# A piece of quantised weights, three fills and two splits change places in the order of work of a four-layer kernel

## What is computed

```python
# layer 0: matrix memory attention, q = layernorm(x), k = v = context
itilde = einsum(gate_in, Wi_w) + Wi_b
ftilde = einsum(gate_in, Wf_w) + Wf_b
csum   = cumsum(log_sigmoid(ftilde))
Dtilde = (csum[i] - csum[j], masked) + itilde[j]
D      = exp(Dtilde - max(Dtilde))
C      = (q @ k.T) * D / TAU
H      = (C @ v) / (max(|sum(C)|, exp(-max)) + 1e-6)
x      = x + tanh(g) * groupnorm(H)
# layer 1, feed-forward: three weight matrices, quantised in blocks of 32 to 4 bits and back
s  = max(|w|) / 7 ;  wq = round(w / s) * s
# layer 2 and 3: attention with 16 heads of 8, whose operands are split into f16 parts
```

## Time and profile before

| | us |
|---|---|
| median of 3 runs | 549.97 (548.64 to 550.31) |
| the profiled execution, its own time | 548.92 |
| the span of that execution, first to last instruction | 546.8 |
| mean granted clock of TensorE | 0.874 |
| critical chain: share of PE, DVE, ACT, POOL | 49%, 27%, 9%, 7% |

### The profile page before, as it was taken

One profiled execution on the slowest core, in us unless ns is written; L12 is line 12 of the kernel. 1 busy time (PEld: TensorE's weight loads), 2 busy tenths in 40 slices (PEclk: granted clock), 3 DMA queues, 4 the chain that ended last, 5 costly groups with the idle time before them and its releaser, 6 DMA issues.

```text
span 546.8 us, 11355 instructions
## 1 busy us (share of the span) xinstructions
PE 421.6 (77%) x4145; PEld 264.0 (48%) x4145; DVE 382.1 (70%) x1061; ACT 320.0 (59%) x656; POOL 234.1 (43%) x364
## 2 busy tenths in 40 slices
PE   3637754999895680049999989986999998889886
PEld 3524421656563330035655666663456656666432
DVE  7766994866876767867666675978786687586441
ACT  2339973656453167247876767663576568778250
POOL 4613896365766908226311111344845662311100
PEclk9999885999998585569999978787899999889787
DMA  7840006400000000000000000000000000000000
GB/s 205 200 36 2 2 2 201 94 1 2 1 1 0 1 0 0 0 1 2 1 2 1 3 2 2 1 2 1 2 1 0 3 1 2 1 3 1 2 19 19
DMA packets 26001, 11.27 MB, mean 21 GB/s; under 512 B 16358, under 2 KB 22876, under 8 KB 25948
## 3 DMA queue, kind: packets, MB, share of 16 engines
q1 hardware_dynamic: 25948, 10.56, 7.8%
HBM read 10.03 MB, written 0.52 MB: 19 GB/s over the span
## 4 chain that ended last, share of the span: by engine, by line
PE 49%; DVE 27%; ACT 9%; POOL 7%; issue 5%; SPq 1%; DMA 1%; DVEq 0%; ACTq 0%
PE psum L709 10%; PE psum L891 6%; PE psum L876 4%; PE psum L877 4%; PE psum L878 3%; DVE qs L1704 3%; POOL work L638 2%; PE psum L1073 2%; PE psum L1007 2%; ACT phase L1098 2%; POOL rstd L566 2%; DVE z L1319 2%; PE psum L716 2%; PE psum L982 2%; ACT phase L1272 2%
## 5 line engine op out<-in xcount | busy, mean ns | idle before, releaser
L638 POOL TENSOR_TENSOR work<-work 128x512 f16<-128x512 f32 x64 | 72.8, 1161 | 43.9 <-ACT work L1158 43.8
L564 POOL TENSOR_SCALAR vr<-mv 128x1 f32<-128x1 f32 x80 | 17.9, 223 | 158.1 <-DVE mv L1313 157.2
L1704 DVE TENSOR_REDUCE qs<-psum 128x4 f16<-128x512 f32 x96 | 59.6, 688 | 7.8 <-PE psum L982 7.7
L1098 ACT ACTIVATE phase<-psum 128x1024 f16<-128x1024 f16 (+1 forms) x52 | 47.5, 933 | 19.3 <-PE psum L709 10.5
L1213 ACT ACTIVATE work<-psum 128x512 f32<-128x512 f32 x64 | 37.5, 596 | 35.7 <-PE psum L878 31.0
L1596 DVE TENSOR_TENSOR work<-work,psum 128x512 f32<-128x512 f32 x64 | 42.7, 684 | 18.5 <-ACT work L1213 16.1
L1272 ACT ACTIVATE phase<-psum 128x512 f32<-128x512 f32 x96 | 49.8, 610 | 4.8 <-PE psum L1007 4.1
L876 PE MATMUL psum<-zTh,split 128*128 128x512 f16 x128 | 51.1, 399 | 1.4 <-POOL zTl L643 1.0
L891 PE MATMUL psum<-wout,work 128*128 128x128 f16 x768 | 47.7, 219 | 4.5 <-POOL work L638 4.2
L877 PE MATMUL psum<-zTl,split 128*128 128x512 f16 x128 | 51.1, 399 | 0.0
L878 PE MATMUL psum<-zTh,split 128*128 128x512 f16 x128 | 51.0, 398 | 0.0
(11 more groups left out here) (339 smaller groups left out, 973.9 us busy)
## 6 DMA issues: line engine op xcount, KB each, us to landing
stage_f<-in_L_ffn_W_in SPq DMA_DIRECT2D x1, 2048.0 KB, 9.5
stage_f<-in_L_ffn_w SPq DMA_DIRECT2D x1, 2048.0 KB, 8.7
x<-in_x SPq DMA_DIRECT2D x1, 512.0 KB, 4.2
c<-in_ctx SPq DMA_DIRECT2D x1, 512.0 KB, 5.5
w<-in_L_ffn_W SPq DMA_DIRECT2D x2, 256.0 KB
out<-x SPq DMA_DIRECT2D x8, 64.0 KB, 1.6
phase<-in_L_ffn_w_up SPq DMA_DIRECT2D x1, 192.0 KB
phase<-in_L_ffn_w_gate SPq DMA_DIRECT2D x1, 192.0 KB
```

The costliest lines, as they stand in the source:

```text
L638: ch.do(pool.tensor_tensor(hidl[:, n % 2, k, :], act[:, n % 2, k, :], hidh[:, n % 2, k, :], ALU.subtract), sem("hid_low"))
L1098: ch.do(A(out, view(u), ACT.Copy), banks.freed(stage, b, name))
L1704: ch.do(v.tensor_reduce(groups(qs[:, b, :, 3 * DA:3 * DA + 1], 4)[:, j], u, AX.X, ALU.max, negate=True), free_of(stage, b, f"s{j}"))
```

## The change

The third item of w8 gets turn 3.7 in place of 2, which puts it behind `x0_score 1`. `x0_split` becomes a chain of its own, with items 0 and 1 ahead of `x0_forget`. The three fills of `qs` and `ks` move from `x0_split 0` to the setup, ahead of the fills of `magic` and `ones`.

```diff
+    "xs": ["x0_split"],
-    "x0": ["x0_split", "x0_stack", "x0_score", "x0_value", "x0_back", "x0_group", "f0_z", "f0_t"],
+    "x0": ["x0_stack", "x0_score", "x0_value", "x0_back", "x0_group", "f0_z", "f0_t"],
...
-    "w8": [(i, i, 0) for i in range(3)],
+    "w8": [(0, 0, 0), (1, 1, 0), (2, 3.7, 0)], "xs": [(0, -0.36, 0), (1, -0.34, 0)] + [(b, b, 0) for b in range(2, NB)],
...
+                    ch.do(v.memset(qs[:, :, :, 3 * DA:4 * DA], 0.0))
+                    ch.do(v.memset(ks[:, :, :, 3 * DA + 1:4 * DA], 0.0))
+                    ch.do(v.memset(ks[:, :, :, 3 * DA:3 * DA + 1], 1.0), sem("stacks_filled"))
                     ch.do(v.memset(magic[:, :], MAGIC))
                     ch.do(v.memset(ones[:, :], 1.0), sem("ones_ready"))
                 elif stage == "x0_split":
-                    if b == 0:
-                        ch.do(v.memset(qs[:, :, :, 3 * DA:4 * DA], 0.0))
-                        ch.do(v.memset(ks[:, :, :, 3 * DA + 1:4 * DA], 0.0))
-                        ch.do(v.memset(ks[:, :, :, 3 * DA:3 * DA + 1], 1.0), sem("stacks_filled"))
```

More of the change, by code:

```diff
@@ L77 @@
     "s0": [(e, e, 0) for e in range(NE)], "so": [(e, e, 0) for e in range(NE)], "s2": [(e, e, 0) for e in range(NE)],
-    "w8": [(i, i, 0) for i in range(3)], "u1": [((c, g), FPS * c + g, 0) for c in range(3) for g in range(FPS)],
+    "w8": [(0, 0, 0), (1, 1, 0), (2, 3.7, 0)], "xs": [(0, -0.36, 0), (1, -0.34, 0)] + [(b, b, 0) for b in range(2, NB)], "u1": [((c, g), FPS * c + g, 0) for c in range(3) for g in range(FPS)],
 }
@@ L112 @@
 }
-PERIOD = {"n0": 1.0, "s0": 0.9, "w8": 1.29, "x0": 1.0, "s2": 1.26, "f0": 1.5,
+PERIOD = {"n0": 1.0, "s0": 0.9, "w8": 1.29, "x0": 1.0, "xs": 1.0, "s2": 1.26, "f0": 1.5,
           "so": 0.5, "x1": 0.38, "u1": 0.62, "x2": 1.26, "f2": 1.95, "x3": 1.44}
```

## The result

The changed kernel is slower: 552.81 us (median of 20 executions) against 549.25 (20), ratio 1.0082, 95% interval 1.0052 to 1.0113. That is 4.5 us by the ratio and 3.6 by the medians; 4.1 were forecast. The profiled execution has a span of 551.6 us, 4.8 more than the one of before.

The account below looks back on a forecast made before the run. It took a chain of waits in the first 60 us as the bound, no engine being full. 0.95 + 0.03 + 2.6 + 1.5 - 1.0 = 4.1 us over the median 549.97 gave 554.1, range 551.5 to 556.1.

Parts of the forecast that it names:

- the likeliest case: Whole kernel: the delay as worked out, 3.4 to 5.4 us, thus 553.4 to 555.4; chance 0.75.
- Fills: At the setup: the moved fills shift statistics and gates by 1.8 us, bounds 0 to 1.8, covered by the load.
- Splits: Ahead of x0_forget on DVE: two splits, 1.3 us, fit into its 1.68 us wait for PE and cost nothing there.
- 3.6 us of cover: Ahead of the biases: slack 39.8 - 36.2 that hides the shifts from early fills and splits.
- more: Stacks 1 and 2: low clock lasts or the two shifts outgrow the cover; 6 us, 556.0, chance 0.08.
- The load as floor: Step w1 on PE: its last load holds the biases, so they gain only 1.0 us, bounds 0 to 1.3.
- The price of the piece: Between score 1 and stack 2: the piece takes DVE 2.6 us, then 1.5 to ACT's stack, bounds 1.1 to 1.85.
- It reaches the end: Behind stack 2: ACT, DVE and POOL have no slack, so the full 4.1 us goes to the end.
- The rival that the load is no floor: Step w1: the load lands before 34 us, the gain is 4.9, the sum -0.2, time 549.8; chance 0.03.
- g: At the biases: the gain in their start, limited by the load; taken as 1.0 us, bounds 0 to 1.3.
- The rival that DVE's idle time soaks the piece up: Around score 1: DVE's idle 1.48 + 1.20 us absorbs the piece's 2.6, leaving the 1.0 gain; 549.0, chance 0.08.
- The receipt: Last load of step w1: a receipt behind the last byte, most of about 2 us, would bring the gain nearer 0.

Follow-up runs that it names:

- e2: The second experiment: the kernel before with only the third w8 piece moved behind score 1, fills and splits unmoved; 554.49 us against 547.62, ratio 1.0136.
- e1: The first experiment: the changed kernel with the third weight piece back at turn 2, fills and splits still early; 549.41 us against 547.62 for before.
- e4: The changed kernel with step w1 (transpose, product needing the load, bias rows) behind the first block's groups; 550.89 us against 547.62 for before, ratio 0.9968.
- e3: The changed kernel with the third piece's DVE work back at turn 2 and only its transpose late; 547.47 us against 547.62 for before, ratio 0.9979.
- e5: The changed kernel with the third piece's DVE work at turn 2, its transpose late and step w1 late; 546.31 us against 548.19 for before, ratio 0.9965.
- e7: The changed kernel with throwaway PE matmuls, 5 in the wait for the load and 10 in the wait for the third piece; 551.06 us against 548.19 for before.
- e8: The changed kernel run again without any edit; 552.89 us against 548.19 for before, ratio 1.0089.
- e6: The changed kernel with the third piece's DVE work at turn 2, its transpose, step w1 and the fills late; 543.72 us against 548.19 for before.

## Why the prediction was right

Its forecast of 554.1 was 4.1 over before; measured is 4.5 by the ratio, within the likeliest case's 3.4 to 5.4. The median itself, 552.81, lies 1.3 under the forecast: inside the range of 551.5 to 556.1, but under the 553.4 at which the likeliest case began, since before has a median of 549.25 over 20 executions and not 549.97. The chances for slower add up to 0.89, not to the 0.88 that it gives.

At stack 2 its sum can be redone with what was measured: 0.95 + 0.03 + 2.61 + 1.90 - 0.92 = 4.57, where it had 0.95 + 0.03 + 2.6 + 1.5 - 1.0 = 4.1. Two sizes were off. The hand-over behind the piece was 0.4 larger. The gain at the load was 0.8 larger at the biases, but had shrunk to 0.92 by the end of score 1, and that this is so near the 1.0 taken is luck. Point by point:

- **Fills.** 1.8 us taken, 2.03 measured at the statistics (6.20 to 8.23). Hidden by the load, as said: in the changed kernel PE still waited 2.38 us for it. The second experiment agrees, without early fills and splits its last norm lies 0.10 from that of the changed kernel. The 0.05 us of the first says nothing on this, since the load ends no wait there.
- **Splits.** `x0_forget` was forecast at 21.3 and came at 21.51. The gates were done near 21.0 on PE, but DVE came out of the first piece 2.4 us later than before and not 1.8 (20.17 against 17.78, part of it in longer `z` instructions, 2.52 against 2.22), so the 1.34 of splits outlasted the wait by about 0.3: they cost a little there, not nothing. The end of ln was forecast at 24.9 and came at 24.73. But DVE took it up only at 26.88: the second piece's multiply took 2.51 us there in place of 0.56 (the same instruction at 21.16 in the kernel before). I had not foreseen that. On the other side the running maximum took 0.42 where it had taken 1.20, so that `am_ready` came at 33.37 and not at 32.9. The 3.6 us of cover were already reckoned behind both shifts, so the prediction's "more" counts them twice where it speaks of shifts that outgrow 3.6. Of them 2.4 were there: this is what PE waited for the load.
- **The load as floor.** Right: the wait is named in the profile, and without it the block ends 1.5 us sooner (e4), or 0.8 beside e3 (e5). The gain at the biases was 1.80 us and not 1.0, because the load came earlier. From the issue of the last load to the product it took 1.99 us (35.34 to 37.33), in e2 1.92, in e7 1.89; from these, as an estimate, the load of the execution of before, with its issue at 36.13, would have let the product run near 38.05, where I had put it. The issue itself moves between executions, from 35.34 to 36.31. The bound "not before about 37.8" held for the execution it was read from and not for the next, and the product ran 0.5 ahead of it. The prediction also took the way from the biases through score 1 to be as long as before; it was 0.87 longer (5.36 against 4.49), with PE at its half pace. At the end of score 1 on DVE 46.63 against 47.55 leaves 0.92 of the gain.
- **The price of the piece.** Right in place and size: DVE had it from 46.66 to 49.27 (46.5 to 49.2 forecast). The step from there to ACT's stack was 1.90, where I had taken 1.5 and bounded 1.85, with PE at its half pace. The prediction expected the wait for the piece to bring the pace down. In the profiled execution it had never risen; in e8 it had, and fell during the wait, and the step took 1.89.
- **It reaches the end.** 4.57 at stack 2, 4.56 at the first group norm, 4.55 at the last norm, and the first expert matmul at 94.93 against 90.38 (the prediction gives 90.6 for before).
- **The rival that the load is no floor** named g = 5 as the point at which nothing is lost; e4, without the floor, had stack 2 still 2.07 later than before and the last norm 3.07. Even then the piece costs more than the freed time gives, and the rival's 4.9 of gain did not last: score 0 on DVE came 4.92 earlier (38.06), score 1 only 3.43 (42.83 against 46.26). The second copy of stack 0 and the exp behind it are the next floor.
- **The rival that DVE's idle time soaks the piece up** falls for its new place (a 4.05 us wait of DVE stands behind the piece there) and is right for its old one: in e3 the same instructions cost nothing where DVE waits for the load.
- **The receipt.** The Trainium skill (DMA: Bandwidth & Descriptors, Anatomy of one DMA) has the signal trail the last byte and gives most of about 2 us to that; the section is on DMAs that GpSimd issues, and this one is SP's. Here it shows as 0.3 to 0.5 us: traffic ends between 36.8 and 37.0, and the product runs at 37.33. It did not bring g near 0, and the measurement decides.

Open: why single kernels' totals differ by 1 to 2 us from what their first block shows (e1 above, e7 below), and e6 by more than 3 us. The granted clock of the stretches behind 300 us differs from execution to execution; no run here changed it on purpose. Open too is what decides when PE's pace rises in the first block: two executions of the same code differ in it.

## What to carry to other kernels

Before work is taken off an engine's path, look up what ends the wait behind it: here the third piece was nearly free in its old place because a load, unseen in the chain, would have held three engines there anyway, until about 1 us before the piece let them go (an estimate: 38.05 + 2.02 against 41.14). Work put between two steps of a pipeline that hands over from engine to engine costs its own time, the hand-over to the next engines and the overlap that was there, here 4.6 us for 2.6 us of arithmetic. A step that others need only in a later layer should not stand, with its wait, ahead of the steps that go on.

## What the runs showed of the hardware

While POOL does its 128x1024 addition of two SBUF operands, one DVE instruction stretches until 0.2 to 0.4 us behind the end of that addition (spans on POOL are rough). In the kernel before it is the scan of the running maximum (1.20 us, 0.42 in the changed kernel):

```profile
25.07 1.20 DVE L1468 TENSOR_TENSOR_SCAN mT<-aT 64x128 f32<-64x128 f32 x1
```

```profile
23.65 2.34 POOL L611 TENSOR_TENSOR x<-x,rows 128x1024 f32<-128x1024 f32 x1
```

In the changed kernel's timeline it is the multiply by `w8r` (2.51 us, 0.56 elsewhere), beside an addition from 23.01 to 25.35; in the second execution of the same code the rounding that follows it (2.38 us, 0.36 elsewhere):

```profile
23.23 0.56 DVE L1433 TENSOR_TENSOR phase<-phase,w8r 128x384 f32<-128x384 f32 x1
23.82 2.38 DVE L1435 TENSOR_SCALAR phase<-phase 128x384 f32<-128x384 f32 x1
```

and on POOL at the same time:

```profile
23.26 2.72 POOL L612 TENSOR_TENSOR x<-x,rows 128x1024 f32<-128x1024 f32 x1
```

There the multiply had begun 0.03 us ahead of the addition and kept its 0.56, and it was the addition that took longer, 2.72 in place of 2.34. Not every instruction is touched: in the kernel before, three short ones that read PSUM stand inside the addition on DVE, from 23.89 on, and take their usual 0.21 to 0.28.

The Trainium skill (GPSIMD Engine Reference, Specifications) says that POOL shares SBUF interfaces with the vector engine, with contention for vector instructions that have two SBUF inputs or run in a two-port mode. The multiply and the scan have two SBUF inputs. The rounding has one; its 0.36 us against the multiply's 0.56 for the same size would fit a faster mode, but no row names the mode, and no run here took the addition away.

The pace of PE can't be read from the granted clock at the start of the program. In all profiles here it is given as 1.00 up to 44 us, while pairs of 128x512 products take 1.03 us as well as 0.60. Where the pace has risen once and falls again, as behind 47 us in e2 and e8, it does read 0.50. In the changed kernel's first profile the pace had not risen by then, and it reads 1.00 for transposes that take the same 1.06 us.
